# One list of 135 tiles in place of two of 71 for a sparse mixture of experts, its second part ordered by token group

## The reference

```
x = x + tanh(g_xattn[0]) * attention_16_heads(layernorm(x), ctx)
x = x + tanh(g_ffn[0])   * mixture_of_6(layernorm(x))       # top 2 of 6 experts, computed densely
x = x + tanh(g_xattn[1]) * attention_1_head(layernorm(x), ctx)
x = x + tanh(g_ffn[1])   * mixture_of_8(layernorm(x))
```

```
logits = x @ Wg                                   # 8 experts
probs  = softmax(top_2(logits))
for e in range(8):
    h = silu(x @ W1[e]) * (x @ W2[e])             # 256 hidden numbers
    out += (h @ W3[e]) * weights[..., e][..., None]
```

## Time and profile before

| | us |
|---|---|
| median of 3 runs | 909.94 |
| the profiled execution | 908.92 |
| its span, first to last instruction | 907.1 |
| first transpose of the tile loop (L1873) starts | 595.0 |
| last transpose of the tile loop starts | 875.6 |
| last scatter is issued | 883.86 |
| first pair load after the loop is issued | 886.28 |

### The profile page before, as it was taken

How to read it: one execution, slowest core, us unless ns; L and a number is a source line. 1 busy time by engine, 2 the same in 40 slices (tenths; PEclk the granted TensorE clock), 3 DMA queues, 4 the chain that set the end, 5 groups by cost and what they waited for, 6 DMA issues and landing times. The chain is left out here.

```text
span 907.1 us, 26462 instructions
## 1 busy us (share of the span) xinstructions
PE 777.2 (86%) x8408; PEld 600.7 (66%) x8408; DVE 690.6 (76%) x2993; ACT 568.8 (63%) x1209; POOL 469.1 (52%) x505
## 2 busy tenths in 40 slices
PE   4999999999999889998998987876887888888870
PEld 2566666666666557676676665766787777788870
DVE  3989889888998968888887877455676565668764
ACT  3777777777777566878888775354354454455430
POOL 3554445444555012377777766645555555555560
PEclk9999999999999989999999999688899999999995
DMA  9101000010000020011111111311223322246638
GB/s 243 43 23 43 20 20 20 27 34 20 20 20 2 3 59 10 13 51 46 42 52 45 49 45 40 89 49 49 68 78 86 90 70 79 76 122 171 176 91 280
DMA packets 62329, 58.12 MB, mean 64 GB/s; under 512 B 10327, under 2 KB 52216, under 8 KB 62232
## 3 DMA queue, kind: packets, MB, share of 16 engines
q1 hardware_dynamic: 44664, 34.42, 14.3%
q0 software_dynamic: 8640, 17.84, 5.7%
q10 hardware_dynamic: 8928, 4.70, 1.8%
HBM read 32.91 MB, written 24.02 MB: 63 GB/s over the span
## 5 line engine op out<-in xcount | busy, mean ns | idle before, releaser
L1132 POOL DMA_INDIRECT contributions<-v_heads,d_token x142 | 137.9, 971 | 105.6 <-PE bc_bank L1882 67.9
L1863 PE MATMUL bc_bank<-d_xT,d_w 128*128 128x128 f32 x1136 | 161.6, 287 | 35.6 <-DVE d_xT L1381 30.1
L1863 PEld LDWEIGHTS bc_bank<-d_xT,d_w 128*128 128x128 f32 x1136 | 143.0, 197 | 46.1 <-DVE d_xT L1381 37.6
L1116 POOL DMA_INDIRECT sorted_rows<-r_send,r_slots x128 | 126.7, 990 | 47.3 <-issue 40.3
L1640 ACT ACTIVATE b_hidden<-bc_bank 128x256 f32<-128x256 f32 x142 | 54.5, 384 | 143.8 <-PE bc_bank L1863 126.5
L494 POOL TENSOR_SCALAR a_k_heads<-a_kT,first 128x512 f32<-128x512 f32 x60 | 93.1, 1569 | 0.8 <-ACT a_kT L547 0.8
L1634 ACT COPY d_w<-w 128x512 f32 x142 | 87.1, 614 | 4.2 <-issue 1.9
L412 DVE TENSOR_REDUCE a_neg_max<-a_scores 128x16 f32<-128x1024 f32 x64 | 78.1, 1221 | 8.1 <-PE a_scores L663 6.9
L571 ACT ACTIVATE a_probs<-a_scores 128x1024 f32<-128x1024 f32 x64 | 65.6, 1025 | 29.5 <-PE a_scores L673 29.4
L578 ACT COPY a_probsT<-a_probsT_bank 128x512 f32<-128x512 f32 x128 | 74.8, 584 | 13.4 <-PE a_probsT_bank L690 12.8
L690 PE MATMUL a_probsT_bank<-first,a_probs 128*128 128x128 f32 x512 | 79.7, 278 | 2.2 <-ACT a_probsT L578 0.3
(11 more groups left out here) (213 smaller groups left out, 1894.1 us busy)
## 6 DMA issues: line engine op xcount, KB each, us to landing
d_rows<-sorted_rows SPq DMA_DIRECT2D x142, 65.0 KB
X<-in_x SPq DMA_DIRECT2D x16, 256.0 KB, 3.1
b_hidden<-contributions SPq DMA_DIRECT2D x8, 512.0 KB
b_weighted<-contributions SPq DMA_DIRECT2D x8, 512.0 KB
out_x<-X ACTq DMA_DIRECT2D x16, 256.0 KB
ctxT<-in_ctx_T SPq DMA_DIRECT2D x16, 192.0 KB, 3.0
c_ctxT<-in_ctx_T SPq DMA_DIRECT2D x16, 192.0 KB
contributions<-v_heads,d_token POOLq DMA_INDIRECT x142
```

The source lines that it names most:

```text
L1116: pool.indirect_dma_start(dispatch.rows, bass.IndirectOffsetOnAxis(ap=slots[n % 2][:, k, j:j + 1], axis=0), send[n % 2][k][:, j, :], None) ...
L1132: pool.indirect_dma_start(dispatch.contributions, bass.IndirectOffsetOnAxis(ap=token[:, t % KEEP:t % KEEP + 1], axis=0), shares[t % KEEP], ...
L1863: last = pe.matmul(uv[m % 2][:, bass.ts(i, P)], w12[m % 3][:, bass.ts(i, P)], xT[m % 4][:], start=True, stop=True)
```

## The change

There is one list with one region for each expert, 128 + 7 = 135 tiles. The first 57 (`EARLY_TILES`, 64 - 7) are taken from the full tiles that the first 8 groups have filled; they are planned as before by `plan_early`, with `is_ge` in place of `is_gt`, and need no filling. The other 78 are ordered by "cells": what each expert has left of its tiles when group 8, then 9, and so on to 15 has been sent. Their plan, `plan_late`, uses 128 partitions, one for each cell, and two products on PE (`find_late`) that add up, over the cells, each tile's row and expert. All rows of group g are then in the first 8(g+1)+8 tiles (`blocks_kept(2 * max(g, 7) + 4)`), and 14 groups (`CLOSED`) are closed behind tiles, only two after the loop. A pair is loaded each 3.5 tiles from n = 87, and 56 pieces are added in steps 86 to 134.

```diff
-HALF_TILES = 2 * GH * GW // P + E1 - 1
-DTILES = HALVES * HALF_TILES
+EARLY_TILES = 2 * GH * GW // P - (E1 - 1)
+DTILES = 2 * G * GW // P + E1 - 1
+LATE_TILES = DTILES - EARLY_TILES
...
+    def plan_late(self, dve, c, part, found):
+        if 0 < part < self.LATE_STEPS:
+            dve.wait_ge(self.plan_step, self.EARLY_STEPS + part)
+        if part == 0:
+            dve.tensor_copy(self.end_row[:], self.next_row[0:1, G])
+            ins = dve.tensor_tensor(self.cell_count[:], self.next_row[:, GH:G + 1, :], ..., ALU.subtract)
+        elif part == 1:
+            dve.tensor_scalar(self.rounded[:, 0], self.cell_count[:, 0], 1.0 / P, -HALF_LESS, ALU.mult, ALU.add)
+            ins = dve.tensor_scalar(self.rounded[:, 1:], self.cell_count[:], 1.0 / P, HALF_LESS, ALU.mult, ALU.add)
...
+        elif part == 6:
+            ins = dve.tensor_reduce(self.cell[:], self.masked[:], AX_X, ALU.add)
...
+    def find_late(self, pe, c, found):
+        pe.wait_ge(self.plan_step, self.EARLY_STEPS + self.LATE_STEPS)
+        pe.matmul(found[:, 0], self.cell_offset[:], self.outside[:], start=True, stop=True)
+        pe.matmul(found[:, 1], c.cell_expert, self.outside[:], start=True, stop=True)
...
-    PAIRS_AT, ADDS_AT = 104, 108
+    CLOSED = G - 2
+    PIECES = 4 * CLOSED
+    PIECES_AT, FIND_AT = 86, 30
+    def pair_step(g):
+        return 87 + 7 * g // 2
+    def piece_step(i):
+        return PIECES_AT + 7 * i // 8
+    def store_step(g):
+        return piece_step(4 * g + 3) + 4
...
-            for first in (0, 4):
-                dispatch.fill_up(sp, 0, first)
...
-                if t in (48, 56):
-                    dispatch.fill_up(sp, 1, (t - 48) // 2)
-                if t == HALF_TILES // 4 * 4:
+                if t in (40, 48):
+                    dispatch.fill_up(sp, (t - 40) // 2)
+                if t == EARLY_TILES // 4 * 4:
                     sp.wait_ge(dispatch.planned, 2)
...
-                if t == PAIRS_AT:
-                    blocks_kept(sp, HALF_TILES // 4 + 1)
-                if PAIRS_AT <= t < PAIRS_AT + 4 * GH:
-                    load_pair((t - PAIRS_AT) // 4)
-            blocks_kept(sp, BLOCKS)
-            for g in range(GH, G):
+                    for g in range(CLOSED):
+                        if pair_step(g) == n:
+                            blocks_kept(sp, 2 * max(g, GH - 1) + 4)
+                            load_pair(g)
+            for g in range(CLOSED, G):
+                blocks_kept(sp, min(2 * g + 4, BLOCKS))
                 load_pair(g)
```

More of the change, by code:

```diff
@@ L857, in __init__ @@
+        self.tile_row = sb("plan_tile_row", [1, DTILES + 1], I32)
         self.plan_step, self.planned = sem("plan_step"), sem("planned")
         self.filled = sem("filled")
-    def plan(self, dve, c, h, part):
+        self.cell_count = sb("plan_cell_count", [P, G - GH + 1, E1], F32)
+        self.rounded = sb("plan_rounded", [P, G - GH + 2, E1], F32)
+        self.bounds = sb("plan_bounds", [P, BOUNDS, E1], F32)
+        self.lengths = sb("plan_lengths", [P, BOUNDS * E1], F32)
+        self.masked = sb("plan_masked", [P, 3, BOUNDS * E1], F32)
@@ L872, in plan @@
         elif part == 3:
-            ins = dve.tensor_reduce(self.tiles[:], self.over[:], AX_X, ALU.add)
+            ins = dve.tensor_tensor(self.upto[:], self.tiles[:].unsqueeze(1).broadcast_to([1, E1, E1]), c.up_to[:], ALU.mult)
         elif part == 4:
-            ins = dve.tensor_tensor(self.upto[:], self.tiles[:].unsqueeze(1).broadcast_to([1, E1, E1]), c.up_to[:], ALU.mult)
+            ins = dve.tensor_reduce(self.ends[:], self.upto[:], AX_X, ALU.add)
         elif part == 5:
-            ins = dve.tensor_reduce(self.ends[:], self.upto[:], AX_X, ALU.add)
+            ins = dve.tensor_tensor(self.past[:], c.tile_number[:].unsqueeze(2).broadcast_to([1, EARLY_TILES, E1]),
+                                    self.ends[:].unsqueeze(1).broadcast_to([1, EARLY_TILES, E1]), ALU.is_ge)
@@ L883, in plan @@
         elif part == 8:
-            ins = dve.tensor_tensor(self.past_tiles[:], self.past[:], self.tiles[:].unsqueeze(1).broadcast_to([1, HALF_TILES, E1]),
-                                    ALU.mult)
+            ins = dve.tensor_reduce(self.start[:], self.past_tiles[:], AX_X, ALU.add)
         elif part == 9:
-            ins = dve.tensor_reduce(self.start[:], self.past_tiles[:], AX_X, ALU.add)
+            ins = dve.tensor_tensor(self.first_f[:], c.tile_number[:], self.start[:], ALU.subtract)
@@ L907, in fill_up @@
             skip_runtime_bounds_check_because="counts end within their regions")
         for i in range(4):
-            sp.dma_start(self.rows[bass.ds(ends[i], P), :], self.fill[:, h * FILLS + first + i]).then_inc(self.filled, 16)
+            sp.dma_start(self.rows[bass.ds(ends[i], P), :], self.fill[:, first + i]).then_inc(self.filled, 16)
     def four_tiles(self, engine, entries, t, largest):
@@ L1026, in group_added @@
     def group_added(eng, g):
-        eng.wait_ge(added, 4 * min(g + 1, GH) + 2 * max(g + 1 - GH, 0))
+        eng.wait_ge(added, 4 * min(g + 1, CLOSED) + 2 * max(g + 1 - CLOSED, 0))
     def store_group(eng, g):
@@ L1051, in _ @@
                 if n == 1:
-                    for h in range(HALVES):
-                        sp.dma_start(dispatch.rows[h * SORTED + E1 * REGION:(h + 1) * SORTED, :].rearrange("(a p) d -> p a d", p=P),
-                                     dispatch.fill[:, h * FILLS + E1:(h + 1) * FILLS]).then_inc(dispatch.filled, 16)
-            for first in (0, 4):
-                dispatch.fill_up(sp, 0, first)
+                    sp.dma_start(dispatch.rows[E1 * REGION:SORTED, :].rearrange("(a p) d -> p a d", p=P),
+                                 dispatch.fill[:, E1:FILLS]).then_inc(dispatch.filled, 16)
             for t in range(0, DTILES, 4):
@@ L1424, in _ @@
                 dve.memset(plan[:, DTILES:], 0)
+            dve.memset(dispatch.bounds[:, 0], 0.0)
+            dve.memset(dispatch.lengths[:, CELLS:], 1000.0)
             for t in ctxT:
@@ L1510, in _ @@
             for t in range(17, DTILES + OUT):
-                if t - 17 <= dispatch.PLAN_STEPS:
-                    dispatch.plan(dve, c, 1, t - 17)
+                if t - 18 < dispatch.LATE_STEPS and t >= 18:
+                    dispatch.plan_late(dve, c, t - 18, found)
+                if t == FIND_AT + 2:
+                    dispatch.plan_late(dve, c, dispatch.LATE_STEPS, found)
                 sparse(t)
-            for g in range(GH, G):
+            for g in range(CLOSED, G):
                 add_group(g)
@@ L1640, in sparse @@
                     act.activation(silu[m % 2], uv[m % 2][:, 0:KH * P], ACT.Silu).then_inc(silu_done, 1)
-                g = (t - ADDS_AT - 6) // 4
-                if (t - ADDS_AT) % 4 == 2 and 0 <= g < GH:
-                    store_group(act, g)
+                for g in range(CLOSED):
+                    if store_step(g) == t:
+                        store_group(act, g)
             for i in STEPS:
@@ L1694, in _ @@
                 sparse(t)
-            for g in range((DTILES + HIDDEN - 1 - ADDS_AT - 6) // 4 + 1, G):
-                store_group(act, g)
+            for g in range(G):
+                if g >= CLOSED or store_step(g) >= DTILES + HIDDEN:
+                    store_group(act, g)
         @block.tensor
```

168 lines of the change are left out of this document (107 added, 61 removed).

## The result

The changed kernel took 888.59 us (median of 4 runs, 885.49 to 889.80), the kernel before 909.54 beside it (4 runs). The ratio is 0.976, 95% interval 0.9728 to 0.9792. It is faster by 21 us, and the forecast was 884.4 with a range of 875 to 895. The profiled execution took 885.49 us, the fastest of the four, with a span of 883.7.

What follows compares the result with a forecast made beforehand. No engine was full overall: a tile loop of PE work plus waits, then a 21.0 us tail without PE. Terms -14.4 + 1.5 - 12.1 - 0.5 = -25.5 on 908.92 gave 883.4, plus 1.0 for the median: 884.4, range 875 to 895.

Steps and rivals of the forecast that it cites:

- the slow one: SP's queue in the loop: waits for scatters before six pairs hold up row loads and stop PE, 913 us; chance 0.03.
- third rival: Tile loop: pace follows place in the program, not pieces; all 112 steps at 1.893 us, total 890.7; chance 0.15.
- Seven tiles less: Tile loop after step 22: 112 steps in place of 119, at the two measured paces, -14.4 us.
- Doubled pieces: Steps 86 to 134: 24 more pieces, seven steps with two, each second one sticking out by up to 0.42 us; +1.5 us.
- Tail: Last scatter's landing to the end: one pair load where eight were, 8.9 us in place of 21.0, -12.1 us.
- Plans: Early plan on fewer elements, late plan reshaped with two more PE products: together -0.5 us.
- Row loads and pair loads together: SP's queue in the loop: pair loads and their waits among row loads cost nothing, covered by 8.7 us of rows ahead.
- Better stretch: Closing stretch: all 48 steps at 1.671 us and doubled pieces hidden, -31.3 us, total 878.6; chance 0.25.
- Bound by DVE: Closing stretch: all 24 added pieces show in full, +10.0 us in place of +1.5, total 892.9; chance 0.12.
- Place: Tile loop: the third rival, pace set by place in the program and not by pieces, 890.7 us; chance 0.15.
- SP stands: SP's queue in the loop: waits of 13 us at six pairs delay row loads and PE, 913 us; chance 0.03.

Runs made afterwards that it cites:

- e4: Changed kernel with no group closed in the loop, all 16 after the last scatter: 835.84 us, one run, beside 829.08 for the kernel before.
- e9: Changed kernel with no group closed in the loop and two empty ACT instructions in each of steps 22 to 69: 835.83 us, one run, beside 834.91.
- e0: Changed kernel again, no edit, in a job without pauses: 812.76 us against 834.29 for the kernel before, ratio 0.9748.
- e1: Changed kernel with only 8 groups closed in the loop, one piece a step from step 104: 822.75 us, 10.0 more than the changed kernel beside it.
- e2: Changed kernel with 12 groups closed in the loop, one piece a step from step 86, none doubled: 809.18 us, 3.6 under the changed kernel.
- e3: Changed kernel with each piece adding one column of 128, with loads, waits and stores as they are: 807.42 us.
- second pair: Kernel before and changed kernel, both unedited, profiled in one job of the 911 us kind: 910.57 and 884.43 us, ratio 0.9711.

## Why the prediction was right, point by point

The direction and the two main terms were right, and the time lay in the range. But the range took in every case except the slow one, so that alone says little: 888.59 is 4.2 us from the forecast and 2.1 from the third rival, and the profiled execution, on which the sum was made, happened to be the fastest of its four.

- *Seven tiles less, -14.4 forecast.* The mechanism is right, the size was too large, and this is the term that was mis-sized. The kernel before's last seven steps took 12.15 us; with 1.8 given back, tiles and pieces together brought 10.3, against -12.9 forecast for the two. I had priced steps 86 to 134 at the 1.760 of the stretch with pieces, as if the pieces made it faster. By that, steps 86 to 104 would take 31.7 us without the doubled pieces; they took 35.2, where the kernel before had 33.6 without any piece. So pieces don't bring the better pace to steps 86 to 104, and the long pauses end at the same place, past step 95, in both kernels, though their pieces start 22 steps apart. That speaks for the third rival, the place in the program. It isn't shown that steps 104 to 134 would keep their pace of 1.79 with no closing work at all, since both kernels have pieces there and e4 and e9 met the other kind. The rival forecast -6.6 for tiles and pieces, which was too small on the other side, since it put 1.893 on the last 30 steps too.
- *Doubled pieces, +1.5.* 0.98 where PE is at full pace all the time (e0 against e1, e2, e3). With the pauses there, 86 to 104 took 1.6 and 0.9 more than in the kernel before in the two pairs, and 104 to 134 nothing. The size was right; that a single piece is free in the steps is shown by e4 against e2. I left the way from the last transpose to the last landing at its old 10.5 us, so the sum had no term for what pieces do to POOL: in the kind without pauses its last scatter goes out 10.4 us after the last transpose with full pieces, 8.4 with thin ones (e3) and 8.1 with none (e4).
- *Tail, -12.1.* Measured -13.1 and -11.8 between the last transpose and the end, and -12.7 with the closing alone changed (e1). My load of 3.68 us was 3.19 and my 3.57 for the store 2.75, since I had taken rows of transfers that ran four and eight at a time. By the fit of the Trainium skill (DMA: Bandwidth & Descriptors, "Anatomy of one DMA — SWDGE (gpsimd) path") the estimates were 3.2 and 2.6; this trace agrees with them better than with my rows, though both are of SP's and ACT's queues. Ahead of the landing 0.5 us was lost (11.0 in place of 10.5), and 1.5 in the second pair (12.1 in place of 10.6).
- *Plans, -0.5.* Not seen. Step 22 comes at the same time in the first pair and 4.0 us earlier in the second, and the same kernels' steps 0 to 22 differ by 3 us between runs with the granted clock. No run isolates the plans, so the -0.5 stays an estimate.
- *Row loads and pair loads together, nothing.* Right: the waits of SP for scatters with row loads behind them were 0.4 us in all (3.3 and 2.9 in e0), PE never waited for rows in the profiled run, and e4 without any pair load has the pace of e2 with twelve.
- *Rivals.* "Better stretch" (878.6) is out: steps 86 to 104 got slower with pieces, and 104 to 134 did not change. "Bound by DVE" (892.9) forecast 10.0 us for the 24 added pieces; all 56 together cost the steps 0.98 us (e0 against e4), and the steps up to 134 gave back only 1.8 and 1.4 in the two pairs with pauses. "Place" fits the pace of steps 86 to 104 and is 2 us from the time, with the open end above. "SP stands" is out.

The sum of the measured terms for the profiled pair is -10.3 - 13.1 = -23.4 where -25.5 was forecast; the medians are 21.0 apart in the first measurement, 21.5 at 834 us, and 26.7 in the 911 us job.

## What to carry to other kernels

Before a stretch's pace is used to price new steps, look whether the same steps had it without the work in question; two stretches that differ in place and in work tell nothing of either alone. Work that is put behind the loop with all its transfers costs its whole length there, and one instruction a step in the loop costs the steps nothing as long as it fits the pace of the bounding engine; two in a step show, but by far less than their length. Look at the engines that aren't bounding too: in the runs without pauses the adds on DVE made POOL's scatters longer, and the lag came due behind the loop. Where a pause has no releaser that was late, don't take it for a property of the kernel until runs of another job show it too.

## What the runs showed that I had not expected

The tile loop has two paces, with the same program: 1.89 us a step with pauses of ACT of up to 3.7 us about every seven steps (both read in steps 22 to 86), and 1.46 without them; the kernel before takes 907 to 916 us with them and 829 to 836 without, and nothing in between was seen. All runs of one job were of one kind. The phases ahead of the loop (first transpose at 593 to 596 us with, 578 to 581 without) differ by 15 us. The pauses come at nearly the same tiles in each trace that has them, 29, 36, 42, 49, 56, 64 and so on, with a few apart, which may point to something in ACT's own program, but what it is, and why a chip or a job has it or not, stays open; the runs meant for it met the other kind. Both kinds give the change the same ratio, 0.971 to 0.976.
